# Neighbour attention on one core: the ReLU of the logits moves to GpSimd, the slope to DMA, and 1344 columns of the bar to ScalarE

## The chip, the core and the metric

The program runs on one core of a Trainium2 chip. The metric is the device time of one execution in microseconds. The profile is of one execution on the same chip; its own time stands beside its span.

## The reference

The input x is 32 images of 32 channels and 56 x 56 = 3136 pixels. It is normalised by channel, goes through a convolution with weights of their own at each pixel, and is added to x. What the change touches is the block that follows, on the normalised sum `pts` (3136 points of 32 numbers for each image):

```python
p = pts / norm(pts)
dist = pairwise_distance(p)
_, nn_idx = top_k(-dist, 16)
nbr = pts[nn_idx]
e, e_n = pts @ W_emb + b_emb, nbr @ W_emb + b_emb
logits = leaky_relu(concat(e, e_n) @ W_att + b_att, 0.1)
attn = softmax(logits, over the 16)
agg = sum(nbr * attn)
y = concat(pts, agg) @ W_conv + b_conv
```

A batch normalisation, a ReLU and two additions end it. The logit of a pair is leaky_relu(own + other), where `own` depends on the query alone and `other` on the neighbour alone. Since leaky_relu(v) = 0.1 v + 0.9 max(v, 0) and whatever depends on the query alone drops out of the softmax, a kernel may use 0.1 other + max(0.9 own + 0.9 other, 0), or that less 0.9 own, which is 0.1 other + max(0.9 other, -0.9 own).

## The kernel before

Five stages run one after the other: `normalise_input`, `convolve`, `prepare` (features, unit vectors, and per point the number `share` = 0.1 other), `split_halves`, `attend` and `normalise_output`. Nearly all the time is in `attend`. It has no neighbour lists: for a tile of 128 queries it makes the scores against all 3136 points, finds the 16 best, and gives all other points the weight zero. An image has 25 tiles, so there are 800 tiles, and all engines run the same software pipeline over them (`each_step`). In step s the engines work on these tiles, in the order in which each engine's `body` writes them; each engine takes its instructions strictly in that order, and semaphores join them.

- TensorE scores tile s+1 in two blocks of 1568 columns (L903, L907), adds up a doubt count for tile s (L914), turns the weights of tiles s-3 and s-4 in seven groups (`turn`, L928 and L930; two banks take turns, so a group waits until ScalarE has copied the group two before it), spreads the inverse total (L938) and aggregates tile s-4 (L948). For 7 of an image's 25 tiles it also does the output convolution (L961, L962).
- ScalarE copies the two score blocks (`copy_scores`, L1022), makes the steep part of the logits of tile s+1 from `shares` (`rise`, L1014, a ReLU over 3136 columns), takes the exponential of tile s-1 (L1034) and copies turned groups (L1049).
- VectorE searches the second half of tile s with 7 MAX8 (L1120), masks tile s-1 (`mask`, L1159: logits joined with the bar, and their largest), merges the 14 lists of 8 of tile s into a bound (`merge`, L1181 to L1191, the last of which counts how many scores reach the bound), searches the first half of tile s+1, reads the doubt count (L1126), repairs the tile if the bound is in doubt (L1134 to L1141) and lowers all scores under the bound (`bar`: L1150 for the first 1568 columns, L1151 for the rest, where it also takes in the slope `shares`).
- GpSimd adds the slope `shares` to the first 1568 columns of the logits in two pieces (L875), one beside each of VectorE's searches.
- SP loads an image's data while the one before it is worked on (`load_batch`, 13 transfers), and the features and outputs of four tiles at a time.

`gate(engine, sem, value, passed)` is a wait followed by a semaphore increment. `masked` holds the logits of five tiles, `scores` those of two.

## Time and profile before

| | |
|---|---|
| time, median of 3 runs (lowest to highest) | 11882.48 us (11870.54 to 11883.2) |
| time of the profiled execution | 11878.96 us |
| its span | 11877.3 us |
| VectorE, ScalarE, TensorE, GpSimd busy in the span | 86%, 86%, 75%, 27% |
| moved by DMA in the span | 480.72 MB |

The span is from the first to the last instruction. Busy shares are averages over all stages; the first 1450 us belong to the stages ahead of `attend`, the last 137 us to the one behind it. A group of instructions is told by its line in the kernel, its engine and its tiles.

### The profile page before, as it was taken

The numbers are of one execution on the slowest core, as the hardware profiler recorded it, in microseconds if no ns is written. First come the engines' busy times: TensorE is split into PE (matmuls) and PEld (weight loads), VectorE is DVE, ScalarE is ACT, GpSimd is POOL, SyncE is SP. The second block draws the span as 40 slices with busy tenths as digits, with TensorE's granted clock in tenths as the row PEclk, the third lists the DMA queues.
The fourth block names the chain that finished last, engine by engine and source line by source line (L and its number), as shares of the span: only waits on it lengthen the run. The fifth ranks groups of instructions, "written<-read, shape, count | busy, mean of one in ns | idle before, by whom it ended". The sixth has DMA issues, their size and how long they took to land. (4 is left out here: it accounts for less than half of the span.)

```text
span 11877.3 us, 322193 instructions
## 1 busy us (share of the span) xinstructions
PE 8897.7 (75%) x114762; PEld 6354.6 (54%) x114762; DVE 10249.3 (86%) x23918; ACT 10170.5 (86%) x11593; POOL 3194.5 (27%) x2042
## 2 busy tenths in 40 slices
PE   4885577777777777777777777777777777777775
PEld 3664355555555555555555555555555555555553
DVE  1001599999999999999999999999999999999997
ACT  3332499999999999999999999999999999989986
POOL 1221022222222222222222222222222222222221
PEclk9887799999999999999999999999999999999998
DMA  8666700000000000000000000000000000000003
GB/s 205 172 178 188 223 3 17 17 17 17 17 17 16 17 16 17 17 4 17 17 17 17 17 17 17 17 17 17 17 17 9 12 17 17 17 17 17 17 4 133
DMA packets 220615, 480.72 MB, mean 40 GB/s; under 512 B 139588, under 2 KB 147396, under 8 KB 202436
## 3 DMA queue, kind: packets, MB, share of 16 engines
q1 hardware_dynamic: 196740, 362.84, 12.1%
q0 software_dynamic: 22272, 96.36, 2.6%
q8 instruction: 1023, 16.76, 0.6%
q14 instruction: 580, 4.75, 0.1%
HBM read 353.59 MB, written 105.50 MB: 39 GB/s over the span
## 5 line engine op out<-in xcount | busy, mean ns | idle before, releaser
L875 POOL TENSOR_TENSOR masked<-masked,shares_a 128x784 f32<-128x784 f32 x1600 | 2983.5, 1865 | 7344.5 <-DVE rest L1191 4228.4
L1120 DVE MAX8 found<-scores 128x8 f32<-128x224 f32 x11200 | 3479.7, 371 | 213.9 <-ACT scores L1022 183.4
L1049 ACT ACTIVATE turned_sb<-psum 128x512 f32<-128x512 f32 (+1 forms) x5600 | 2946.4, 573 | 497.2 <-PE psum L928 435.6
L930 PE MATMUL psum<-ident_a,masked 128*128 128x128 f32 x19200 | 2646.9, 282 | 915.9 <-ACT turned_sb L1049 890.7
L930 PEld LDWEIGHTS psum<-ident_a,masked 128*128 128x128 f32 x19200 | 2370.7, 194 | 1370.8 <-issue 1370.5
L1159 DVE CUSTOM_DVE_ANT_0 masked<-masked,scores 128x3136 f32<-128x3136 f32 x800 | 2720.8, 3401 | 0.2 <-DVE scores L1151 0.2
L1022 ACT ACTIVATE scores<-psum 128x1568 f32<-128x1568 f32 x1600 | 2374.4, 1484 | 199.9 <-DVE minus_top L1159 166.2
L1034 ACT ACTIVATE masked<-masked,minus_top 128x3136 f32<-128x3136 f32 x800 | 2363.5, 2954 | 0.0
L1014 ACT ACTIVATE masked<-shares_a,own 128x3136 f32<-128x3136 f32 x800 | 2328.1, 2910 | 1.0
L928 PE MATMUL psum<-ident_a,masked 128*128 128x128 f32 (+1 forms) x10400 | 1759.9, 284 | 533.6 <-ACT turned_sb L1049 500.2
L928 PEld LDWEIGHTS psum<-ident_a,masked 128*128 128x128 f32 (+1 forms) x10400 | 1103.7, 139 | 1292.8 <-issue 1216.2
L903 PE MATMUL psum<-points 32*128 32x392 f32 x12800 | 1543.6, 552 | 28.6 <-DMA rows<-table 16.4
L948 PE MATMUL psum<-turned_sb,rows 128*32 128x128 f32 (+1 forms) x40000 | 1538.8, 282 | 0.5 <-ACT inverse_sb L1030 0.5
L1151 DVE SCALAR_TENSOR_TENSOR scores<-scores,bound,shares_a 128x1568 f32<-128x1568 f32 x800 | 1467.8, 1835 | 0.0
L948 PEld LDWEIGHTS psum<-turned_sb,rows 128*32 128x32 f32 (+1 forms) x40000 | 1148.8, 112 | 271.2 <-issue 174.3
L327 ACT ACTIVATE w_turned<-w_ps 96x384 f32<-96x384 f32 x784 | 348.0, 486 | 592.9 <-PE w_ps L286 588.4
L339 DVE COPY conv_sb<-conv_ps 128x128 f32 x196 | 57.2, 292 | 892.5 <-PE conv_ps L308 892.5
L914 PE MATMUL psum<-ones,above 128*1 128x1 f32 x1600 | 150.8, 163 | 898.0 <-DVE rest L1191 898.0
L1150 DVE TENSOR_SCALAR scores<-scores,bound 128x1568 f32<-128x1568 f32 x800 | 808.6, 1011 | 8.3 <-DVE bound L1141 2.5
L914 PEld LDWEIGHTS psum<-ones,above 128*1 128x1 f32 x1600 | 84.9, 80 | 1156.4 <-issue 1153.3
L903 PEld LDWEIGHTS psum<-points 32*128 32x128 f32 x12800 | 509.7, 186 | 229.2 <-issue 42.8
L907 PE MATMUL psum<-halves_a,minus 3*128 3x392 bf16 x6400 | 566.9, 334 | 0.0
(146 smaller groups left out, 6224.2 us busy)
## 6 DMA issues: line engine op xcount, KB each, us to landing
w_in<-in_L_conv_weight_dram POOLq DMA_DIRECT2D x392, 144.0 KB, 3.4
w_in<-in_L_conv_weight_dram SPq DMA_DIRECT2D x392, 144.0 KB, 3.5
points<-unit SPq DMA_DIRECT2D x128, 392.0 KB
shares_a<-share SPq DMA_DIRECT2D x32, 1568.0 KB
windows<-xg SPq DMA_DIRECT2D x42, 928.0 KB, 13.9
xg<-padded SPq DMA_DIRECT2D x16, 812.0 KB, 18.2
table<-table_sb SPq DMA_DIRECT2D x32, 404.2 KB
rows<-table SPq DMA_DIRECT2D x32, 396.0 KB
```

Source lines behind the costliest of these rows:

```text
L875: nc.gpsimd.tensor_tensor(m, m, shares[:, t.half, k * width:(k + 1) * width], ALU.add).then_inc(logits_ready, 1)
L903: nc.tensor.matmul(ps[:, r * BANK:r * BANK + SCH], points[C * r:C * (r + 1), t.half, t.queries()], points[C * r:C * (r + 1), t.half, at:at ...
L928: last = nc.tensor.transpose(out, block, ident[:])
L930: last = nc.tensor.matmul(out, block, ident[:], start=True, stop=True)
L948: last = nc.tensor.matmul(ps[q:q + C, SUM_BANK:SUM_BANK + P], rows[0:width, t.half, j, 0:C], turned_sb[0:width, t.par, j, :], start=j < PE ...
L1014: nc.scalar.activation(masked[:, t.ring, :], shares[:, t.half, :], ACT.Relu, bias=own[:, t.half, at:at + 1], scale=STEEP / SLOPE).then_inc ...
L1022: nc.scalar.activation(scores[:, t.par, quad * QUAD:(quad + 1) * QUAD].rearrange("p (a b) -> p a b", b=SCH), ps[:, 0:PER * BANK].rearrange ...
L1034: nc.scalar.activation(masked[:, t.ring, :], masked[:, t.ring, :], ACT.Exp, bias=minus_top[:, t.ring:t.ring + 1], scale=-1.0, accum_out=to ...
L1049: nc.scalar.activation(turned_sb[0:high, t.par, g * GROUP:g * GROUP + width // P, :].rearrange("p a b -> p (a b)"), ps[0:high, bank:bank + ...
L1120: n = step(nc.vector.max(found[:, t.par, c, :], scores[:, t.par, c * PART:(c + 1) * PART]))
L1151: nc.vector.scalar_tensor_tensor(high, high, bound[:, 0:1], shares[:, t.half, POOL_COLS:N], ALU.subtract, ALU.min).then_inc(barred, 1)
L1159: nc.vector.tensor_tensor_reduce(m, m, scores[:, t.par, :], -1.0, -NEVER, ALU.add, ALU.min, minus_top[:, t.ring:t.ring + 1]).then_inc(mask ...
```

## The change

GpSimd no longer adds the slope. It makes the logits' steep part itself, from a new per-point row `steep` = 0.9 other that `prepare` stores and SP loads for each image into `steeps` (one buffer, two parts): max(steep, -own) for the first 1792 columns, and its negative, min(-steep, own), for the last 1344, whose `share` and `steep` are stored with the opposite sign. After each of these two operations GpSimd issues a DMA from `shares` that adds the slope into the tile's logits. ScalarE's `rise` is gone. The bar of the last 1344 columns moves from VectorE to ScalarE as a ReLU of bound minus score (`bar_high`); the mask is cut at column 1792 into `mask_low` and `mask_high`; the merge is written out in six calls so that other work stands between them.

```diff
+SPLIT = 4 * CH
@@ prepare: one more row per image in half_sb, stored as steep
-                        nc.tensor.matmul(half_ps[0:2 * PER, c % 4, 0:CH], shares[:], feat_sb[:, par, c * CH:(c + 1) * CH],
+                        nc.tensor.matmul(half_ps[0:ROWS, c % 4, 0:CH],
+                                         shares[:] if c * CH < SPLIT else minus_shares[:], feat_sb[:, par, c * CH:(c + 1) * CH],
@@ attend, SP
+            def load_steep(b, k):
+                cols = SIDES[k]
+                sp.dma_start(steeps[:, cols], steep[bass.ds(b * N + cols.start, cols.stop - cols.start)].partition_broadcast(P)).then_inc(steep_in[k], 16)
...
             def body(tile):
                 here = tile(0)
+                if ends_batch(here):
+                    next_steep(here, 1)
+                if ends_batch(tile(-1)):
+                    next_steep(tile(-1), 0)
@@ attend, GpSimd
-            def add_slope(t, passed):
...
-                    nc.gpsimd.tensor_tensor(m, m, shares[:, t.half, k * width:(k + 1) * width], ALU.add).then_inc(logits_ready, 1)
+            def clamp(t, k):
+                at = t.c if t.c < TILES - 1 else OWN
+                cols = SIDES[k]
+                if k == 0:
+                    nc.gpsimd.tensor_scalar(masked[:, t.ring, cols], steeps[:, cols], -NEVER, minus_own[:, t.half, at:at + 1],
+                                            ALU.min, ALU.max).then_inc(clamped, 1)
+                else:
+                    nc.gpsimd.tensor_scalar(masked[:, t.ring, cols], steeps[:, cols], own[:, t.half, at:at + 1], NEVER,
+                                            ALU.min, ALU.max).then_inc(clamped, 1)
+                gate(pool, clamped, t.count(2, k + 1), pool_passed)
+                pool.dma_start(masked[:, t.ring, cols], shares[:, t.half, cols], accum_op=ALU.add).then_inc(slope_in[t.par], 16)
...
+                if here:
+                    clamp_high(here, tile(1))
+                if coming:
+                    clamp_low(coming, tile(RING - 1), here)
@@ attend, ScalarE
-                nc.scalar.activation(masked[:, t.ring, :], shares[:, t.half, :], ACT.Relu, bias=own[:, t.half, at:at + 1],
-                                     scale=STEEP / SLOPE).then_inc(rises_ready, 1)
+            def bar_high(t):
+                act.wait_ge(settled, t.count(1, 1))
+                s = scores[:, t.par, SPLIT:N]
+                nc.scalar.activation(s, s, ACT.Relu, bias=bound[:, 0:1], scale=-1.0).then_inc(high_barred, 1)
...
                 if older:
                     copy_turned(older, 6)
+                if tile(1):
+                    bar_high(tile(1))
...
-                    rise(coming, tile(RING - 1))
@@ attend, VectorE
-                low, high = scores[:, t.par, 0:POOL_COLS], scores[:, t.par, POOL_COLS:N]
-                step(nc.vector.tensor_scalar(low, low, bound[:, 0:1], 0.0, ALU.subtract, ALU.min))
-                nc.vector.scalar_tensor_tensor(high, high, bound[:, 0:1], shares[:, t.half, POOL_COLS:N],
-                                               ALU.subtract, ALU.min).then_inc(barred, 1)
+                dve.sem_inc(settled, 1)
+                s = scores[:, t.par, 0:SPLIT]
+                nc.vector.tensor_scalar(s, s, bound[:, 0:1], 0.0, ALU.subtract, ALU.min).then_inc(barred, 1)
...
+            def mask_low(t):
+                gate(dve, slope_in[t.par], t.same_par(32, 32), dve_passed)
+                gate(dve, barred, t.count(1, 1), dve_passed)
...
+            def mask_high(t):
+                gate(dve, low_masked, t.count(1, 1), dve_passed)
+                gate(dve, high_barred, t.count(1, 1), dve_passed)
+                m = masked[:, t.ring, SPLIT:N]
+                nc.vector.tensor_tensor_reduce(m, m, scores[:, t.par, SPLIT:N], 1.0, low_top[:, t.par:t.par + 1],
+                                               ALU.add, ALU.min, minus_top[:, t.ring:t.ring + 1]).then_inc(masked_ready, 1)
```

The order of VectorE's instructions in a step of `attend`, from the end of the first search on, before (in brackets the semaphores that an instruction waits for):

```order
L1159 ISA masked,minus_top<-masked,scores 128x3136 [waits a_logits,a_barred]
L1159 ISA minus_top 128x1
L1181 MAX best<-found 128x8 [waits a_chain]
L1183 MATCH_REPLACE rest<-best,found 128x112 [waits a_chain]
L1185 MAX best<-rest 128x8 [waits a_chain]
L1187 SCALAR_TENSOR_TENSOR bound_low<-over,best,margin 128x2 [waits a_chain]
L1189 SCALAR_TENSOR_TENSOR bound<-under,best,bound_low 128x2 [waits a_chain]
L1191 SCALAR_TENSOR_TENSOR rest,above<-found,bound,weight 128x112 [waits a_chain]
```

and in the changed kernel:

```order
L1221 ISA masked,low_top<-masked,scores 128x1792 [waits a_slope0,a_barred]
L1221 ISA low_top 128x1
L1254 MAX best<-found 128x8 [waits a_chain]
L1229 ISA masked,minus_top<-masked,scores,low_top 128x1344 [waits a_low_masked,a_high_barred]
L1229 ISA minus_top 128x1
L1259 MATCH_REPLACE rest<-best,found 128x112 [waits a_chain]
L1243 TENSOR_TENSOR agg<-psum,inverse_sb 128x128 [waits a_summed,a_inverse_in]
L1264 MAX best<-rest 128x8 [waits a_chain]
L1234 RECIPROCAL inverse<-total 128x1 [waits a_exp]
L1269 SCALAR_TENSOR_TENSOR bound_low<-over,best,margin 128x2 [waits a_chain]
L1274 SCALAR_TENSOR_TENSOR bound<-under,best,bound_low 128x2 [waits a_chain]
L1279 SCALAR_TENSOR_TENSOR rest,above<-found,bound,weight 128x112 [waits a_chain]
```

The second mask, with its wait for ScalarE's bar (`a_high_barred`), stands ahead of most of the merge and of the count (L1279). The aggregate's product and the reciprocal, which stood behind the count, now stand ahead of it.

ScalarE in the changed kernel, from the copy of the second score block of one step to the bar of the high side in the next:

```order
L1084 ACTIVATE scores<-psum 128x1568
L1106 REGISTER_ALU
L1111 ACTIVATE turned_sb<-psum 128x512
...
L1111 ACTIVATE turned_sb<-psum 128x512
L1096 ACTIVATE masked,total<-masked,minus_top 128x3136
L1106 REGISTER_ALU
L1111 ACTIVATE turned_sb<-psum 128x512
...
L1111 ACTIVATE turned_sb<-psum 128x512
...
L1111 ACTIVATE turned_sb<-psum 64x128
L1074 ACTIVATE scores<-scores,bound 128x1344
```

The bar (L1074) stands behind the exponential (L1096) and three copies of turned groups; the ReLU over 3136 columns, which stood behind the first score copy, is gone.

TensorE from the doubt count to the second score block of a step, the same in both kernels but for the line numbers, here before:

```order
L914 MATMUL psum<-ones,above 1x1 [waits a_doubt,a_doubts_in]
L37 REGISTER_ALU
L928 MATMUL psum<-ident_a,masked 128x128 [waits a_turned_in]
L928 MATMUL psum<-ident_a,masked 128x128 x3
L938 MATMUL psum<-ident_a,inverse 128x128 [waits a_agg,a_inverse]
L37 REGISTER_ALU
L903 MATMUL psum<-points 128x392 [waits a_scores_in]
L903 MATMUL psum<-points 128x392 x3
L907 MATMUL psum<-halves_a,minus 128x392 x4
```

The doubt product waits for VectorE's count (`a_doubt`), and the second score block stands behind it; nothing moved here.

## Rows read from the trace of the kernel before

**Rows 1.** Busy time by stretch: PE, PEld, DVE, ACT, POOL, PEclk, DMA share, GB/s.

```profile
1450.57:11739.20 10288.63, 7941.34 (x92498) 5612.29 (x92499) 9909.73 (x23244) 9614.67 (x10647) 2978.00 (x1598) 0.97 0.07 15
```

**Rows 2.** One line's instructions: duration min/median/max ns, first and last start.

```profile
L1159 DVE CUSTOM_DVE_ANT_0 masked<-masked,scores x800: 3393/3402/3607, 1450.6 to 11739.2; 128x3136 f32<-128x3136 f32 x160
```

**Rows 3.** In order of time, one step: start us, us, engine, line, [idle before].

```profile
5000.05 3.40 DVE L1159 CUSTOM_DVE_ANT_0 masked<-masked,scores 128x3136 f32<-128x3136 f32 x1
...
5003.69 0.09 DVE L1183 MATCH_VALUE_LOAD rest<-best,found 128x8 f32 x1
...
5004.06 1.47 ACT L1022 ACTIVATE scores<-psum 128x1568 f32<-128x1568 f32 x1
...
5005.15 0.08 DVE L1191 DVE_READ_ACCUMULATOR rest<-found,bound,weight 128x1 f32 x1
...
5005.35 0.15 DVE L1164 RECIPROCAL inverse<-total 128x1 f32<-128x1 f32 x1
...
5005.52 0.19 PE L914 MATMUL psum<-ones,above 128*1 128x1 f32 x2 [1.19 <-DVE rest L1191]
5005.67 0.69 DVE L1120 MAX8 found<-scores 128x8 f32<-128x224 f32 x2 [0.17 <-ACT scores L1022]
...
5007.31 0.35 PE L907 MATMUL psum<-halves_a,minus 3*128 3x392 bf16 x4
...
5008.85 1.50 ACT L1022 ACTIVATE scores<-psum 128x1568 f32<-128x1568 f32 x1
...
5010.20 1.11 ACT L1049 ACTIVATE turned_sb<-psum 128x512 f32<-128x512 f32 x2
...
5011.16 2.96 ACT L1034 ACTIVATE masked<-masked,minus_top 128x3136 f32<-128x3136 f32 x1
...
5012.56 3.40 DVE L1159 CUSTOM_DVE_ANT_0 masked<-masked,scores 128x3136 f32<-128x3136 f32 x1
...
5014.05 1.37 ACT L1049 ACTIVATE turned_sb<-psum 128x512 f32<-128x512 f32 x3
```

**Rows 4.** Groups by line, 5000 to 6000 us: xcount | busy us, mean ns | idle before.

```profile
L875 POOL TENSOR_TENSOR masked<-masked,shares_a 128x784 f32<-128x784 f32 x157 | 292.8, 1865 | 710.2 <-DVE rest L1191 411.8 <-DVE scores L1151 298.5
...
L1014 ACT ACTIVATE masked<-shares_a,own 128x3136 f32<-128x3136 f32 x78 | 227.0, 2910 | 0.1
...
L1151 DVE SCALAR_TENSOR_TENSOR scores<-scores,bound,shares_a 128x1568 f32<-128x1568 f32 x78 | 143.1, 1834 | 0.0
...
L1150 DVE TENSOR_SCALAR scores<-scores,bound 128x1568 f32<-128x1568 f32 x78 | 78.8, 1010 | 0.9 <-DVE bound L1141 0.5
```

**Rows 5.** Groups by line, ScalarE, whole span.

```profile
L1005 ACT ACTIVATE own<-rows,att_bias 128x1 f32<-128x1 f32 x32 | 9.3, 292 | 0.0
```

**Rows 6.** In order of time, a step behind a repaired tile.

```profile
5156.08 0.08 DVE L1191 DVE_READ_ACCUMULATOR rest<-found,bound,weight 128x1 f32 x1
...
5156.46 0.19 PE L914 MATMUL psum<-ones,above 128*1 128x1 f32 x2 [14.21 <-DVE rest L1191]
...
5159.61 0.55 PE L907 MATMUL psum<-halves_a,minus 3*128 3x392 bf16 x4
...
5160.28 1.48 ACT L1022 ACTIVATE scores<-psum 128x1568 f32<-128x1568 f32 x1 [0.91 <-PE psum L907]
```

**Rows 7.** In order of time, TensorE around 3467 us.

```profile
3466.93 2.05 PE L930 MATMUL psum<-ident_a,masked 128*128 128x128 f32 x8 [3.02 <-ACT turned_sb L1049]
```

**Rows 8.** Busy time by stretch, two stretches.

```profile
3466.30:3473.10 6.80, 6.17 (x30) 4.48 (x31) 4.73 (x12) 1.71 (x4) 1.84 (x1) 0.50 0.02 5
...
5145.70:5162.70 17.00, 6.19 (x40) 4.40 (x44) 15.65 (x34) 7.35 (x8) 5.01 (x3) 0.50 0.00 0
```

**Rows 9.** Groups by line, GpSimd, whole span.

```profile
L862 POOL TENSOR_SCALAR_AFFINE_SELECT ident_a<-ident_a 128x128 f32<-128x128 f32 x1 | 0.3, 290 | 73.6 <-DVE own_feat L1091 73.6
```

**Rows 10.** DMA: a queue's packets, MB, share of 16 engines; an issue's KB, us to landing.

```profile
q0 software_dynamic: 22272, 96.36, 2.6%
...
x_sb<-conv POOLq DMA_DIRECT2D x8, 1568.0 KB, 10.4
```

More of the change, by code:

```diff
@@ L342, in _, with prepare @@
             each_half(dve, body)
-def prepare(nc, x, conv, bias, W_emb, W_att, feat, unit, base, half_sq, share, table):
+def prepare(nc, x, conv, bias, W_emb, W_att, feat, unit, base, half_sq, share, steep, table):
     conv_rows, base_rows = conv.rearrange("b c n -> (b c) n"), base.rearrange("b c n -> (b c) n")
@@ L434, in _ @@
                     sp.dma_start(share[rows].rearrange("(b n) -> b n", n=N), half_sb[PER:2 * PER, :]).then_inc(stored[par], 16)
+                    sp.dma_start(steep[rows].rearrange("(b n) -> b n", n=N), half_sb[2 * PER:ROWS, :]).then_inc(stored[par], 16)
             for par in range(2):
@@ L681, in each_step, with attend @@
         fixed(s)
-def attend(nc, feat, unit, pieces, share, table, W_emb, b_emb, W_att, b_att, W_conv, b_conv, y):
+def attend(nc, feat, unit, pieces, share, steep, table, W_emb, b_emb, W_att, b_att, W_conv, b_conv, y):
     BANK = 512
@@ L829, in next_batch, with next_steep, ends_batch @@
                 load_batch(t.batch(1, 1), 1 - t.half)
+            def load_steep(b, k):
+                cols = SIDES[k]
+                sp.dma_start(steeps[:, cols], steep[bass.ds(b * N + cols.start, cols.stop - cols.start)].partition_broadcast(P)).then_inc(steep_in[k], 16)
+            def next_steep(t, k):
+                gate(sp, clamped, t.count(2, k + 1), sp_passed)
+                load_steep(t.batch(1, 1), k)
+            def ends_batch(t):
+                return t and t.c == TILES - 1 and not (isinstance(t.i, int) and t.at > ALL - TILES)
             def load_features(t):
@@ L854, in _ @@
             load_batch(0, 0)
+            for k in range(2):
+                load_steep(0, k)
             each_step(sp, body)
@@ new lines, in clamp_high, with clamp_low @@
+            def clamp_high(t, passed):
+                if t.c == 0:
+                    gate(pool, steep_in[1], t.batch(16, 16), pool_passed)
+                if passed:
+                    gate(pool, barred, passed.count(1, 1), pool_passed)
+                clamp(t, 1)
+            def clamp_low(t, used, beside):
+                if t.c == 0:
+                    gate(pool, steep_in[0], t.batch(16, 16), pool_passed)
+                    gate(pool, own_ready, t.batch(4, 4), pool_passed)
+                if used:
+                    gate(pool, turned, used.count(T_GROUPS, T_GROUPS), pool_passed)
+                if beside:
+                    gate(pool, doubt_ready, beside.count(1, 1), pool_passed)
+                clamp(t, 0)
@@ L881, in _ @@
+            def body(tile):
+                here, coming = tile(0), tile(-1)
+                if here:
+                    clamp_high(here, tile(1))
+                if coming:
+                    clamp_low(coming, tile(RING - 1), here)
             each_step(pool, body)
@@ L1186, in merge, with set_bound @@
                 dve.wait_ge(chain, n)
-                n = step(nc.vector.scalar_tensor_tensor(bound_low[:], over[:], last, margin[:], ALU.mult, ALU.subtract))
+                return step(nc.vector.scalar_tensor_tensor(bound_low[:], over[:], last, margin[:], ALU.mult, ALU.subtract))
+            def set_bound(n):
                 dve.wait_ge(chain, n)
-                n = step(nc.vector.scalar_tensor_tensor(bound[:], under[:], last, bound_low[:], ALU.mult, ALU.min))
+                return step(nc.vector.scalar_tensor_tensor(bound[:], under[:], last, bound_low[:], ALU.mult, ALU.min))
@@ L1190, in merge, with count_above @@
+            def count_above(t, n):
                 dve.wait_ge(chain, n)
-                nc.vector.scalar_tensor_tensor(rest[:], found_all, bound[:, 1:2], weight8[:].rearrange("p a b -> p (a b)"),
+                nc.vector.scalar_tensor_tensor(rest[:], found_of(t), bound[:, 1:2], weight8[:].rearrange("p a b -> p (a b)"),
                                                ALU.is_ge, ALU.mult, accum_out=above[:, 0:1]).then_inc(doubt_ready, 1)
             def body(tile):
-                here, coming = tile(0), tile(-1)
+                here, coming, passed = tile(0), tile(-1), tile(1)
@@ L1196, in body @@
                 if here:
                     n = search(here, 1)
-                if tile(1):
-                    mask(tile(1))
+                if passed:
+                    mask_low(passed)
                 if here:
-                    merge(here, n)
+                    n = top_first(here, n)
+                if passed:
+                    mask_high(passed)
+                if here:
+                    n = drop_first(here, n)
                 if tile(NORM_LAG):
                     normalise(tile(NORM_LAG))
+                if here:
+                    n = top_second(n)
@@ L1204, in body @@
                 if tile(3):
                     invert_total(tile(3))
+                if here:
+                    n = lower_bound(n)
+                    n = set_bound(n)
+                    count_above(here, n)
                 if coming:
@@ L1341, in build @@
     feat, unit = (nc.dram_tensor(name, [C, BATCH * N], FP32).ap() for name in ("feat", "unit"))
-    half_sq, share = (nc.dram_tensor(name, [BATCH * N], FP32).ap() for name in ("half_sq", "share"))
+    half_sq, share, steep = (nc.dram_tensor(name, [BATCH * N], FP32).ap() for name in ("half_sq", "share", "steep"))
     pieces = nc.dram_tensor("pieces", [3, BATCH * N], BF16).ap()
```

109 lines of the change are left out of this document (58 added, 51 removed).

## The prediction

> **What bounds the kernel now.** I read the busy times of the searches first, then the line of the mask, then one regular step in order of time. In the 10,289 us from the first mask to the last VectorE is busy 9,910 us (96%), ScalarE 9,615 (93%), TensorE 7,941 (77%) at a granted clock of 0.97 [rows 1]. The mask on VectorE runs once a step, 800 times, from 1450.6 to 11739.2 us [rows 2]: 799 steps of 12.88 us. One regular step is 12.51 us, from one mask's start to the next, 5000.05 to 5012.56 [rows 3]. The 799 regular steps would take 9,995 us; the other 293 us are repairs, loop ends and batch changes. What lies around the steps is 11,879 (the profiled execution's own time, 3.5 us below the median shown, 11,882.5) minus 10,289, so 1,590 us.
>
> In the regular step VectorE waits 0.17 us for the copied scores and TensorE 1.19 us for the count that VectorE makes [rows 3]. VectorE is the bound, with ScalarE close behind. Of what ScalarE makes in the same step VectorE needs only the score copies. That is what the change alters.
>
> **The change on each engine by itself.** VectorE loses the second half of the bar (1.83 us [rows 4]). Its first half grows from 1568 to 1792 columns, 1.01 x 224/1568 = +0.14 us. The mask is cut in two, one more fixed part of some 0.08 us. From 12.51 - 0.17 that leaves 12.34 - 1.83 + 0.14 + 0.08 = 10.7 us. ScalarE loses the 2.91 us ReLU over 3136 columns and gains one over 1344. Pro rata that is 1.25 us; a one-column activation costs 0.29 us [rows 5], so with the fixed part 0.29 + (2.91 - 0.29) x 1344/3136 = 1.41 us. Ends 1.25 and 1.41; I take 1.41, as these activations have the fixed part. If only these sums counted, the step would fall by 1.7 us.
>
> **The chain that closes.** The new ScalarE order puts the bar of the high side behind the exponential and three copies; the new VectorE order puts the second mask, which waits for that bar, ahead of the rest of the merge and the count; TensorE still waits for the count before the second score block; and ScalarE copies that block before the exponential. So a bar at the head of one ScalarE step leads through VectorE, TensorE and ScalarE to the bar of the next step, and each link waits for the one before it. Its length is the step's least time:
>
> - bar of the high side, 1.41 us;
> - hand-over ScalarE to VectorE, 0.14 us: the copy that begins at 5004.06 ends 1.47 us later, the search starts at 5005.67 [rows 3];
> - second mask to the next instruction, 3.40 x 1344/3136 = 1.46 us [rows 2];
> - from the replace's first part to the count's end, 5003.69 to 5005.15 + 0.08 = 1.54 us, and now also the aggregate's product and the reciprocal that stood behind it (5005.15 to 5005.67 less the 0.17 wait, 0.35 us). They fill gaps of the dependent merge; I keep 0.30 of it: 1.84 us [rows 3];
> - count's end to the end of the second score block on TensorE, 5005.23 to 5007.31 + 0.35 = 2.43 us [rows 3];
> - hand-over TensorE to ScalarE, 0.12 us: 5159.61 + 0.55 to 5160.28 [rows 6];
> - ScalarE: score copy, two turned copies, exponential, three turned copies: 5008.85 to 5014.05 = 5.20 us, and 1.37 us for the three copies less the 0.15 by which an activation starts before the end of the one ahead (5008.85 + 1.50 against 5010.20): 6.42 us [rows 3].
>
> The sum is 13.82 us a step against 12.51. VectorE stands idle in it for some 3 us, between its two masks. Neither the second mask nor anything behind it on VectorE (searches, doubt test, low bar) can pass that wait.
>
> **TensorE's clock on the chain.** From the end of its second turn until the count TensorE has nothing to do. That wait began at 5005.52 - 1.19 = 5004.33; the three copies that stand ahead of the new bar ended a step's 12.51 us before 5014.05 + 1.22, at 5002.76 [rows 3]. Of those 1.57 us I take 1.5. From the bar's start the count takes 1.41 + 0.14 + 1.46 + 1.84 us and TensorE's own start 0.29 (5005.23 to 5005.52). The pause becomes 5.14 - 1.5 = 3.6 us, from 1.19. Before, a wait of 3.02 us [rows 7] was followed by a stretch at 0.50 of the clock, the 1.2 GHz level, that lasted 6.8 us [rows 8]. At that level the link from count to score block takes 5156.08 + 0.08 to 5159.61 + 0.55 = 4.00 us [rows 6, 8], 1.57 more than 2.43. Nothing of it is hidden: in that step ScalarE waits 0.91 us for the block [rows 6]. In 18 of 25 steps nothing fills the pause (in 7 the output convolution stands there), so I charge 18/25 x 1.57 = 1.13 us. Bounds: 0 and 1.57. Step: 13.82 + 1.13 = 14.95 us.
>
> **What I cost at nothing.** GpSimd's two clamps replace two additions of 1.87 us [rows 4]. No row has this operation over these widths. From above, the two-input addition's 2.38 ns a column gives 4.3 and 3.2 us; a one-input operation over 128 columns takes 0.29 us [rows 9], so, if 0.1 us of it is fixed, 1.5 ns a column, 2.8 and 2.1 us, which I take. The first lies beside the second search, the other beside the first search, and VectorE's 3 idle us cover an overrun. The two accumulating DMAs add 128 x 3136 x 4 bytes = 1.606 MB a step. GpSimd's queue moved 96.36 MB in 2.6% of the span of 16 engines, 309 us [rows 10], so plain copying costs 5.15 us a step; one such transfer of 1568 KB took 10.4 us to land beside others. No row shows an accumulating one: below 5.15 there is no reason; above, anything under 15 us is hidden, as a tile's DMAs start over a step before its mask. I take twice, 10.3 us. The Trainium skill ("Collectives: The Full Stack", the bandwidth ceiling) says an add inside a DMA reads two sources and so runs at half the copying rate; by it the price would be this 10.3 us and the sum the same, and it speaks against the fourth case below; no run here shows it. The steep rows are 1.6 MB per batch in front of the batch loads in SP's queue; their cover is the step between a batch's last clamp and the next first one, and uncovered they would cost 32 x 10.4 = 333 us. The two further small activations per batch (0.3 us each) fall into ScalarE's wait for the score block.
>
> **The sum.** 1,590 + 293 + 799 x 14.95 = 13,828 us. I keep the 293 us whole, though VectorE's idle time will swallow part of them. That is 1,949 us above the profiled execution.
>
> **The rivals.**
>
> 1. *The chain holds, the clock doesn't fall.* For it: score blocks and turns still give TensorE some 9 us of work a step. Against it: the fall behind a 3.02 us wait [rows 7, 8]. 1,883 + 799 x 13.82 = 12,925 us.
> 2. *Faster: the chain doesn't close*, because the high bar is ready before VectorE asks. VectorE's 10.7 us then set the step: 1,883 + 799 x 10.7 = 10,432 us. It decides if ScalarE runs ahead by more than the 3 us by which the bar comes late in my sum, that is, if count to score block and exponential to bar together were 3 us shorter than their rows. Only the sums by engine speak for it.
> 3. *The clamps hold VectorE up.* If a clamp and a VectorE operation on two inputs exclude each other, and the clamps cost the upper price, then low bar 1.15 (1.01 x 1792/1568), clamp 3.2, mask 1.94, maximum 0.3, mask 1.46, merge 1.84, clamp 4.3 and two hand-overs of 0.14 follow each other: 14.5 us, 1,883 + 799 x 14.5 = 13,469 us, with no share of the clock's in it. At the price that I take they come to 11.9 us and decide nothing. The Trainium skill ("SBUF — State Buffer", who interferes with whom) states this lock: whichever starts first holds the shared port for its whole instruction. In the traces so far no clamp-like operation overlaps a two-input one for long, so nothing shows it.
> 4. *The accumulating DMAs set the step.* Point of decision: 14.95/5.15, 2.9 times the copying price. At four times it, 20.6 us a step, 18,342 us. For it: no such transfer was ever seen here.
>
> **How the numbers follow.** The forecast gets 0.62, the first rival 0.20, the second 0.04, the third 0.05, the fourth 0.09. Forecast at its clock bounds: 13.82 to 15.39, which is 12,925 to 14,180 us; errors of 0.2 us in the chain add 160 us on either side. The range 12,750 to 14,400 us holds the forecast, rivals 1 and 3, and leaves out rivals 2 and 4. This kernel's runs differ by 0.1%, so 0.2% (24 us) is about what can be told from no change. Faster by more than that: rival 2, 0.04. Same: 0.01, if errors cancel. Slower: 0.95.
>
> **What would show it.** Right: ScalarE waiting for the score block with 1.5 us or more before the second score copy; VectorE waiting 2 to 4 us before the second mask, released by the high bar; TensorE waiting 3.5 to 4.5 us before the doubt product; a mean granted clock in the searches below 0.9; a step of 14.5 to 15.5 us. Wrong: a step under 12.5 us with VectorE busy throughout (rival 2); a wait before the first mask that the DMA ends (rival 4); masks or bars stretched beyond the durations here (rival 3); the clock at 0.97 as before, and a step near 13.8 (rival 1).

## The result and the profile after

The changed kernel takes 14,166.9 us, median of 4 runs (14,157.99 to 14,183.73), against 11,882.8 (11,870.54 to 11,888.83) for the kernel before, run beside it: 1.1925 times as long, 95% interval 1.1905 to 1.1946, or 2,284 us more. The prediction was slower, 13,828 us, with a range that holds the time. The profiled execution took 14,157.99 us.

First the searches as a whole, from the first low mask to the last, as [rows 1] shows them for before:

```profile
core 0: us, PE busy (x) PEld busy (x) DVE busy (x) ACT busy (x) POOL busy (x), PEclk, DMA share, GB/s
1455.30:14014.40 12559.10, 9618.03 (x92440) 6722.86 (x92440) 8600.81 (x24042) 8588.39 (x10707) 3940.57 (x3192) 0.82 0.58 119
```

VectorE did shed the work that the change takes from it: 8,601 us instead of 9,910. So did ScalarE: 8,588 instead of 9,615. Over 799 steps that is 10.76 and 10.75 us a step. Yet the stretch is 2,270 us longer. VectorE and ScalarE are each busy 68% of it, TensorE 77% (9,618 us, part of them at a lower clock). No engine is busy throughout; something makes them wait for each other. The mask's line, which answers to [rows 2], gives the step:

```profile
engine op xcount: duration ns min/median/max, first and last start us, forms
L1221 DVE CUSTOM_DVE_ANT_0 masked<-masked,scores x800: 2001/2006/2027, 1455.3 to 14014.4; 128x1792 f32<-128x1792 f32 x160
```

(14,014.4 - 1,455.3) / 799 = 15.72 us a step, 12.88 before. The waits of the whole run, longest first, say who waits for whom (engine, line waited at, releaser, us in total, times, longest):

```profile
POOL masked L908 <- DVE rest L1279: 7435.3, 799, 16.1
...
PE psum L975 <- DVE rest L1279: 2589.1, 800, 16.5
DVE masked L1229 <- ACT scores L1074: 2202.1, 785, 10.2
...
ACT scores L1084 <- PE psum L968: 1346.2, 802, 17.9
```

Read as arrows these close a ring. VectorE's second mask (L1229) waits for ScalarE's bar (L1074); TensorE's doubt product (L975) waits for VectorE's count (L1279); ScalarE's score copy (L1084) waits for TensorE's score block (L968); and the bar stands behind that copy in ScalarE's order. Each of the three waits occurs some 800 times, about once a step. The first line looks worst and costs nothing here: GpSimd is early and has time.

The ring can be followed through two steps in order of time (start, duration, engine, line; in brackets the idle time before and what ended it):

```profile
6000.89 1.62 DVE L1229 CUSTOM_DVE_ANT_0 masked<-masked,scores,low_top 128x1344 f32<-128x1344 f32 x1 [3.20 <-ACT scores L1074]
...
6003.95 0.08 DVE L1279 DVE_READ_ACCUMULATOR rest<-found,bound,weight 128x1 f32 x1
...
6004.33 0.19 PE L975 MATMUL psum<-ones,above 128*1 128x1 f32 x2 [3.66 <-DVE rest L1279]
...
6006.43 0.57 PE L968 MATMUL psum<-halves_a,minus 3*128 3x392 bf16 x4
...
6007.18 1.48 ACT L1084 ACTIVATE scores<-psum 128x1568 f32<-128x1568 f32 x1 [1.44 <-PE psum L968]
...
6013.85 1.40 ACT L1074 ACTIVATE scores<-scores,bound 128x1344 f32<-128x1344 f32 x1
...
6015.44 1.62 DVE L1229 CUSTOM_DVE_ANT_0 masked<-masked,scores,low_top 128x1344 f32<-128x1344 f32 x1 [2.36 <-ACT scores L1074]
...
6018.50 0.08 DVE L1279 DVE_READ_ACCUMULATOR rest<-found,bound,weight 128x1 f32 x1
...
6018.88 0.19 PE L975 MATMUL psum<-ones,above 128*1 128x1 f32 x2 [3.66 <-DVE rest L1279]
...
6021.75 0.55 PE L968 MATMUL psum<-halves_a,minus 3*128 3x392 bf16 x4
...
6022.50 1.48 ACT L1084 ACTIVATE scores<-psum 128x1568 f32<-128x1568 f32 x1 [1.83 <-PE psum L968]
...
6028.57 0.60 ACT L1111 ACTIVATE turned_sb<-psum 128x512 f32<-128x512 f32 x1 [0.24 <-PE psum L991]
...
6029.83 0.27 ACT L1111 ACTIVATE turned_sb<-psum 64x128 f32<-64x128 f32 x1 [0.67 <-PE psum L989]
6030.01 1.40 ACT L1074 ACTIVATE scores<-scores,bound 128x1344 f32<-128x1344 f32 x1
...
6031.60 1.62 DVE L1229 CUSTOM_DVE_ANT_0 masked<-masked,scores,low_top 128x1344 f32<-128x1344 f32 x1 [3.20 <-ACT scores L1074]
```

The first step, mask to mask, takes 14.55 us, the second 16.16. The links do the same work in both. What differs is TensorE's clock, in the same stretch cut into pieces (columns as above; the clock is the third figure from the end):

```profile
6000.67:6004.33 3.66, 0.00 (x0) 0.03 (x1) 3.37 (x13) 2.35 (x4) 0.07 (x1) 1.00 0.00 0
6004.33:6005.60 1.27, 1.21 (x12) 1.02 (x16) 1.27 (x7) 0.14 (x1) 1.27 (x1) 1.00 0.03 6
6005.60:6008.90 3.30, 3.30 (x20) 2.02 (x16) 1.83 (x4) 1.86 (x3) 1.98 (x3) 0.53 0.16 33
6008.90:6015.15 6.25, 6.24 (x88) 4.75 (x87) 4.17 (x10) 6.08 (x8) 1.62 (x2) 0.98 0.99 196
...
6018.88:6021.75 2.87, 2.81 (x16) 1.73 (x20) 2.87 (x9) 0.28 (x1) 2.29 (x2) 0.60 0.00 0
6021.75:6024.24 2.49, 2.49 (x17) 1.79 (x9) 0.15 (x2) 1.74 (x2) 1.91 (x3) 0.50 0.69 138
6024.24:6028.00 3.76, 3.76 (x60) 3.23 (x60) 3.76 (x8) 3.76 (x5) 0.67 (x1) 0.73 1.11 218
```

In both steps TensorE idles 3.66 us with the clock granted in full. When it works again the clock at first stays at 1.00 (to 6005.60 and beyond in the first step, to 6019.40 in the second) and then falls to 0.50, the 1.2 GHz level; a piece that holds both levels shows their mean. Behind the second pause the low stretch is the longer one: 0.50 until 6026.00, 1.00 again from 6026.30. It slows the aggregate that stands ahead of the turns (L1009, 2.81 us instead of 1.95), so that the turns begin later and ScalarE's copies wait for them.

The new instructions on GpSimd, by group (count, busy us, mean ns, idle before), and its DMA queue (packets, MB, share of 16 engines' span), beside [rows 9, 10]:

```profile
L914 POOL DMA_DIRECT2D masked<-shares_a x1600 | 1423.5, 890 | 974.0 <-POOL masked L908 455.8 <-POOL masked L911 454.7 <-issue 39.0
L908 POOL TENSOR_SCALAR masked<-steeps,minus_own 128x1792 f32<-128x1792 f32 x800 | 1395.8, 1745 | 7462.3 <-DVE rest L1279 7435.3 <-ACT minus_own L1067 27.0
L911 POOL TENSOR_SCALAR masked<-steeps,own 128x1344 f32<-128x1344 f32 x800 | 1151.2, 1439 | 210.7 <-DVE scores L1214 162.1 <-issue 30.9
...
q0 software_dynamic: 252672, 1380.97, 48.1%
```

The clamps take 1.75 and 1.44 us. Together with the DMA issues GpSimd is busy 4.93 us a step. The first mask waits for the adding DMAs 24 us in the whole run.

### The profile page after: what moved, and what is told of

The parts are those of the page before. It is cut to its first block and busy times, and to the rows that moved or that the text cites. A ratio compares the mean times of both kernels' runs of the same rounds, so it can differ in the third digit from the quotient of the medians.

```text
span 14156.3 us, 333305 instructions
## 1 busy us (share of the span) xinstructions
PE 10574.8 (75%) x114762; PEld 7465.9 (53%) x114762; DVE 8939.9 (63%) x24731; ACT 9142.2 (65%) x11658; POOL 4160.9 (29%) x3642
## 5 line engine op out<-in xcount | busy, mean ns | idle before, releaser
L908 POOL TENSOR_SCALAR masked<-steeps,minus_own 128x1792 f32<-128x1792 f32 x800 | 1395.8, 1745 | 7462.3 <-DVE rest L1279 7435.3
L991 PEld LDWEIGHTS psum<-ident_a,masked 128*128 128x128 f32 x19200 | 2844.6, 228 | 888.9 <-issue 886.9
L991 PE MATMUL psum<-ident_a,masked 128*128 128x128 f32 x19200 | 3219.6, 321 | 79.7 <-issue 72.0
L1084 ACT ACTIVATE scores<-psum 128x1568 f32<-128x1568 f32 x1600 | 2352.6, 1470 | 1400.9 <-PE psum L968 1346.2
L1229 DVE CUSTOM_DVE_ANT_0 masked<-masked,scores,low_top 128x1344 f32<-128x1344 f32 x800 | 1294.4, 1618 | 2204.1 <-ACT scores L1074 2202.1
L1096 ACT ACTIVATE masked<-masked,minus_top 128x3136 f32<-128x3136 f32 x800 | 2330.6, 2913 | 0.0
L975 PE MATMUL psum<-ones,above 128*1 128x1 f32 x1600 | 150.6, 163 | 2589.1 <-DVE rest L1279 2589.1
L989 PE MATMUL psum<-ident_a,masked 128*128 128x128 f32 (+1 forms) x10400 | 1872.2, 305 | 257.5 <-ACT turned_sb L1111 200.5
L964 PE MATMUL psum<-points 32*128 32x392 f32 x12800 | 1991.4, 700 | 24.6 <-DMA rows<-table 16.0
L1009 PE MATMUL psum<-turned_sb,rows 128*32 128x128 f32 (+1 forms) x40000 | 1866.3, 328 | 0.5 <-ACT inverse_sb L1092 0.5
L914 POOL DMA_DIRECT2D masked<-shares_a x1600 | 1423.5, 890 | 974.0 <-POOL masked L908 455.8
L989 PEld LDWEIGHTS psum<-ident_a,masked 128*128 128x128 f32 (+1 forms) x10400 | 1202.3, 150 | 942.7 <-issue 850.4
L1221 DVE CUSTOM_DVE_ANT_0 masked<-masked,scores 128x1792 f32<-128x1792 f32 x800 | 1605.5, 2007 | 24.5 <-DMA masked<-shares_a 24.3
L1009 PEld LDWEIGHTS psum<-turned_sb,rows 128*32 128x32 f32 (+1 forms) x40000 | 1409.5, 134 | 389.1 <-issue 300.1
L975 PEld LDWEIGHTS psum<-ones,above 128*1 128x1 f32 x1600 | 91.0, 80 | 2856.6 <-issue 2856.6
L911 POOL TENSOR_SCALAR masked<-steeps,own 128x1344 f32<-128x1344 f32 x800 | 1151.2, 1439 | 210.7 <-DVE scores L1214 162.1
L1074 ACT ACTIVATE scores<-scores,bound 128x1344 f32<-128x1344 f32 x800 | 1122.2, 1403 | 48.0 <-DVEq L1208 48.0
L1214 DVE TENSOR_SCALAR scores<-scores,bound 128x1792 f32<-128x1792 f32 x800 | 902.8, 1128 | 18.8 <-DVE bound L1204 3.1
```

The lines of the kernel that those rows point to most:

```text
L908: nc.gpsimd.tensor_scalar(masked[:, t.ring, cols], steeps[:, cols], -NEVER, minus_own[:, t.half, at:at + 1], ALU.min, ALU.max).then_inc(cl ...
L914: pool.dma_start(masked[:, t.ring, cols], shares[:, t.half, cols], accum_op=ALU.add).then_inc(slope_in[t.par], 16)
L964: nc.tensor.matmul(ps[:, r * BANK:r * BANK + SCH], points[C * r:C * (r + 1), t.half, t.queries()], points[C * r:C * (r + 1), t.half, at:at ...
L989: last = nc.tensor.transpose(out, block, ident[:])
L991: last = nc.tensor.matmul(out, block, ident[:], start=True, stop=True)
L1009: last = nc.tensor.matmul(ps[q:q + C, SUM_BANK:SUM_BANK + P], rows[0:width, t.half, j, 0:C], turned_sb[0:width, t.par, j, :], start=j < PE ...
```

## The experiments

All times are medians; ratios are to the kernel before, run beside them. Every diff is against the changed kernel, unless it says otherwise.

### The change without its last part

The bar of the high side returns to VectorE; the rest of the change stays.

```diff
@@ ScalarE
-                if tile(1):
-                    bar_high(tile(1))
@@ VectorE, bar
-                dve.sem_inc(settled, 1)
+                s = scores[:, t.par, SPLIT:N]
+                nc.vector.tensor_scalar(s, s, bound[:, 0:1], 0.0, ALU.subtract, ALU.min).then_inc(high_barred, 1)
@@ VectorE, mask_high: the sum times -1 instead of 1; prepare and clamp: the high side's sign as the low side's
```

> The high bar goes back to VectorE, behind the low bar's place (all logits with one sign, all of the mask as a sum times -1); clamps, adding DMAs and the cut mask stay. It is the change without its last part. Theory: VectorE gets some 0.87 us more a step, 11.5, and loses the wait; the loop second search to count 7.6, score block 2.4, score copy 1.5, hand-overs 0.4 gives 11.9 us, more if the clock falls: 11,100 to 11,900 us. If the clamps or the DMAs cost the time and not the bar on ScalarE: 13,500 us or more.

Measured: 11,665.6 us, ratio 0.9821 (0.9806 to 0.9836). Clamps on GpSimd and slope by DMA are a gain of 209 us (1.8%) over the kernel before that ran beside it (11,874.6), clear of the noise. The last part of the change, the bar on ScalarE, is what costs: 14,167 - 11,666 = 2,501 us.

### The clock alone

```diff
             def add_doubts(t):
+                for _ in range(10):
+                    nc.tensor.matmul(ps[96:P, Y_BANK:Y_BANK + P], ident[:, 0:C], ident[:], start=True, stop=True)
                 gate(pe, doubt_ready, t.count(1, 1), pe_passed)
```

> Ten extra products of the identity (128 x 32 by 128 x 128), whose result nobody reads, stand on TensorE ahead of the doubt product, where it waits 3.66 us for the count; all else as in the change. Theory (chain and clock are two terms): granted clock over 0.95, the links from count to score block and ScalarE's turned copies back at full-clock values, step 1.40 + 0.19 + 1.54 + 1.60 + 2.43 + 0.18 + 6.42 = 13.76 us, 12,600 to 12,900 us in all. If the clock costs nothing on the chain: 14,100 to 14,200 us. If the clock stays at the low level all the same, the ten products take longer than the wait and the time rises, by up to 500 us.

Measured: 13,014.6 us, ratio 1.0951 (1.0933 to 1.0969). Ten products more a step, and 1,152 us less. In this kernel the lines behind the insertion have numbers two higher. One step in order of time:

```profile
6009.39 1.40 ACT L1076 ACTIVATE scores<-scores,bound 128x1344 f32<-128x1344 f32 x1
...
6010.98 1.62 DVE L1231 CUSTOM_DVE_ANT_0 masked<-masked,scores,low_top 128x1344 f32<-128x1344 f32 x1 [2.14 <-ACT scores L1076]
...
6014.05 0.08 DVE L1281 DVE_READ_ACCUMULATOR rest<-found,bound,weight 128x1 f32 x1
...
6014.43 0.19 PE L977 MATMUL psum<-ones,above 128*1 128x1 f32 x2 [1.21 <-DVE rest L1281]
...
6016.22 0.35 PE L968 MATMUL psum<-halves_a,minus 3*128 3x392 bf16 x4
...
6016.76 1.48 ACT L1086 ACTIVATE scores<-psum 128x1568 f32<-128x1568 f32 x1 [0.92 <-PE psum L968]
...
6023.21 1.40 ACT L1076 ACTIVATE scores<-scores,bound 128x1344 f32<-128x1344 f32 x1
...
6024.80 1.62 DVE L1231 CUSTOM_DVE_ANT_0 masked<-masked,scores,low_top 128x1344 f32<-128x1344 f32 x1 [2.14 <-ACT scores L1076]
```

And the whole of its searches:

```profile
1464.00:12878.10 11414.10, 9664.41 (x108444) 7231.44 (x108448) 8620.65 (x24042) 8518.64 (x10709) 4019.49 (x3192) 0.98 0.64 131
```

The clock is 0.98 instead of 0.82, and the step from mask to mask is 24.80 - 10.98 = 13.82 us, with VectorE's wait for the bar still there. So the ring is there without the clock's fall, and the fall comes on top. The total lies 115 us above the range expected: the mean step is 11,414 / 799 = 14.29 us. Most of the 0.47 us over the regular step are irregular steps, which I had left almost out. The rest are the products themselves. In the 218 of the 799 steps in which the output convolution (L1024, L1025 here) stands ahead of the doubt product, TensorE has no pause left to fill, the products run past the count, and the step takes 14.27 us in the median instead of 13.82: some 100 us in all. So the 1,152 us are what the products save on balance, and the clock's fall cost some 100 us more than that (an estimate from these steps).

### What the adding DMAs cost

First they were left out, then they copied instead of adding.

```diff
-                pool.dma_start(masked[:, t.ring, cols], shares[:, t.half, cols], accum_op=ALU.add).then_inc(slope_in[t.par], 16)
+                pool.sem_inc(slope_in[t.par], 16)
```

> The accumulating DMAs of the slope are left out (1600 in all, 1.28 GB), so the logits lack their part 0.1 other; GpSimd frees their waiters itself. Theory: the first mask waits for these DMAs 24 us in the whole run, so nothing changes by more than 30 us: 14,130 to 14,200 us. If the DMAs' traffic slows the engines or holds the step: below 13,900 us.

```diff
-                pool.dma_start(masked[:, t.ring, cols], shares[:, t.half, cols], accum_op=ALU.add).then_inc(slope_in[t.par], 16)
+                pool.dma_start(masked[:, t.ring, cols], shares[:, t.half, cols]).then_inc(slope_in[t.par], 16)
```

> The 1600 adding DMAs copy instead of adding, so the logits are the slope alone. All else as in the change: it prices the add. If adding reads both sources at half the rate, the queue's share of the 16 engines falls from 48% to about 25% of the span; the trace's plain transfers on this queue ask for 5.15 us a step, 800 x 5.15 / 14,150 = 29%, and some 2% for the earlier stages. Time as in the change within 100 us if the DMAs bind nothing.

Measured: 14,094.0 us without them (1.1866, 1.1846 to 1.1886), and 14,081.1 us with copies (one run). 73 us are more than the 30 expected, but 3% of the loss: the DMAs don't hold the step. The queue line of the copying kernel:

```profile
q0 software_dynamic: 252672, 1380.97, 24.7%
```

The same packets and bytes take half the time. 0.481 x 14,156 less the 309 us of the other stages [rows 10] is 6,500 us, 8.13 us a step; copying, 0.247 x 14,079 - 309 = 3,169 us, 3.96 us a step. An add costs 2.05 copies. The Trainium skill ("Collectives: The Full Stack", the bandwidth ceiling) derives half the rate for the adds of a ring collective, as an add reads two sources; the two runs agree for these DMAs inside one core, with the factor 2.05.

### The bar one step earlier

```diff
@@ ScalarE, body
-                if tile(1):
-                    bar_high(tile(1))
...
+                if tile(0):
+                    bar_high(tile(0))
                 if tile(1):
                     exponentiate(tile(1))
```

> ScalarE's bar of the high side is made one step earlier, just ahead of the exponential, instead of at the head of the next step. Theory: the exponential and three copies leave the path to the second mask. The count still comes behind both masks, so the loop that is left is second search to count 7.6 us, count to score block 2.4, hand-overs 0.4, score copy 1.5: 11.9 us, more where the clock falls. 799 x 12.2 + 1,599 = 11,350 us, between 11,100 and 12,000 us; VectorE's wait before the second mask falls below 0.5 us. If DMA or GpSimd set the step: 14,170 us. If ScalarE now waits for VectorE's doubt test and passes that wait on, over 13,000 us.

Measured: 12,324.9 us, ratio 1.0372 (1.0349 to 1.0395). The wait for the bar is gone, as expected (7 us in all instead of 2,202), and 1,842 us with it. But the time is 325 us over the range. In the trace another wait has grown: TensorE's turns (L989) wait 1,862 us for ScalarE's turned copies, 201 in the change. The copies of the last three groups stand behind the exponential, which now comes later, and TensorE has two banks for seven groups. TensorE is now the late one: it waits for the count (L975) in 62 steps, in the change in 800. The clock is 0.89.

To see how much of that was the clock, the ten products were put into this kernel as well.

> The early bar together with the ten extra products on TensorE. It tells what the early bar's 12,325 us held of clock: theory (the chain left is 11.9 us at full clock, the rest is the clock): 1,599 + 293 + 799 x 11.9 = 11,400 us, between 11,250 and 11,650. If a wait of another kind lengthened it, it stays over 12,000 us.

Measured: 13,404.1 us, ratio 1.1284 (1.1266 to 1.1301), 1,079 us more instead of some 900 less: a clear miss. The trace says why:

```profile
6009.47 0.08 DVE L1281 DVE_READ_ACCUMULATOR rest<-found,bound,weight 128x1 f32 x1
...
6010.29 2.85 PE L973 MATMUL psum<-ident_a 128*32 128x128 f32 x17
...
6012.87 0.19 PE L977 MATMUL psum<-ones,above 128*1 128x1 f32 x2
...
6013.52 0.15 DVE L1191 TENSOR_SCALAR doubts<-psum 1x1 uint32<-1x1 f32 x1 [1.95 <-PE psum L977]
```

The count is ready at 6009.55 and TensorE begins the products only at 6010.29: it comes late from its turns and has no pause ahead of the doubt product here. The products lie on the path: VectorE waits 909 us in all for the doubt product, 91 without them. They raise the clock (0.96) and cost more than that gives. So this run does not tell how much of the early bar's 12,325 us is clock; it tells that TensorE with its turns is on its path.

### The second mask behind the count

This takes the bar out of the path to the count. `bound` needs a second buffer, since ScalarE may still read one tile's bound while VectorE writes the next.

```diff
-        bound = enter(nc.sbuf_tensor("bound", [P, 2], FP32))
+        bound = enter(nc.sbuf_tensor("bound", [P, 2, 2], FP32))
@@ bar, bar_high, set_bound, count_above, settle_doubts: bound[:, t.par, ...]
@@ VectorE, body
-                if passed:
-                    mask_high(passed)
...
                     count_above(here, n)
+                if passed:
+                    mask_high(passed)
```

> Second mask (1344 columns) moved behind the count on VectorE; the bound has two buffers, so that ScalarE's bar of one tile may still read while VectorE writes the next tile's bound. Theory (closed chain): bar 1.40, hand-over 0.19 and second mask 1.54 us leave the path to the count. VectorE's own 10.65 us a step and the loop second search to count (7.6 less 1.6), score block 2.4, score copy 1.5, hand-overs 0.4 (10.3 us) are then the longest; with what ScalarE's order still costs 10.8 to 11.8 us a step, and with 1,599 us outside the steps and up to 293 of irregular ones 10,300 to 11,300 us, below the kernel before. TensorE's wait for the count falls below 2 us, granted clock above 0.95. If the adding DMAs or GpSimd set the step: 14,100 us.

Measured: 11,419.7 us, ratio 0.9615 (0.9602 to 0.9628). One instruction in another place turns 19% slower into 4% faster. It is 120 us above the expected range. Two steps of the second mask and the low clamp:

```profile
6004.97 1.62 DVE L1229 CUSTOM_DVE_ANT_0 masked<-masked,scores,low_top 128x1344 f32<-128x1344 f32 x1
6005.09 3.13 POOL L908 TENSOR_SCALAR masked<-steeps,minus_own 128x1792 f32<-128x1792 f32 x1 [3.00 <-PE psum L991]
...
6017.51 1.75 POOL L908 TENSOR_SCALAR masked<-steeps,minus_own 128x1792 f32<-128x1792 f32 x1 [3.66 <-PE psum L991]
...
6017.62 3.05 DVE L1229 CUSTOM_DVE_ANT_0 masked<-masked,scores,low_top 128x1344 f32<-128x1344 f32 x1 [0.34 <-ACT scores L1074]
```

Both now begin at the count. Whichever is first keeps its own time (1.62 or 1.75 us), and the other takes 1.4 us longer than its own, as if it began when the first had ended. This is the lock of the prediction's third rival, seen for the first time. The Trainium skill ("SBUF — State Buffer", who interferes with whom) describes just this for VectorE with two inputs against a reading GpSimd; the four rows agree.

So the clamp was made to wait for the mask instead of the count (against the late-mask kernel):

```diff
-            def clamp_low(t, used, beside):
+            def clamp_low(t, used, passed):
...
-                if beside:
-                    gate(pool, doubt_ready, beside.count(1, 1), pool_passed)
+                if passed:
+                    gate(pool, masked_ready, passed.count(1, MASKED_FREE + 1), pool_passed)
```

> The late mask, and GpSimd's clamp of the low side waits for the end of the second mask and not for the count. In the late-mask kernel count, clamp and second mask begin together, and of the two one takes its own time and the other 1.4 us more (mask 1.62 and clamp 3.13, or clamp 1.75 and mask 3.05 us); the mask's mean is 1.94 us. Theory (the two exclude each other on the shared memory port): mask back to 1.62 in all steps, low clamp back to 1.75, the 0.32 us a step are VectorE's: up to 256 us less than 11,420, between 11,150 and 11,400 us. If the stretch comes from something else (DMA writes, for one): the mask's mean stays above 1.8 us and the time at 11,420.

```profile
L1229 DVE CUSTOM_DVE_ANT_0 masked<-masked,scores,low_top x800: 1617/1619/1620, 1460.6 to 11247.6; 128x1344 f32<-128x1344 f32 x160
```

All 800 masks are back to 1.62 us, so the lock it was. But the time is 11,384.0 us (0.9588, 0.9575 to 0.9601): 36 us of a possible 256. The rest turned into another wait: VectorE's waits for ScalarE's score copies and bars grew from 475 to 722 us.

That other wait was taken to be ScalarE's, 1.32 us ahead of the second score copy, for a block that itself waits for the first score copy. A turned copy was moved into it (against the clamp-gate kernel):

```diff
+                if past:
+                    copy_turned(past, 2)
                 if coming:
                     copy_scores(coming, 1, tile(1))
                 if past:
-                    copy_turned(past, 2)
                     copy_turned(past, 3)
```

> As the clamp-gate kernel, and on ScalarE the third turned copy stands ahead of the second score copy instead of behind it. In the late-mask kernel ScalarE waits there 1.32 us for the score block, which waits on TensorE for the first score copy (the two blocks share their banks). Theory: ScalarE's order sets what is left over VectorE's 10.65 us; some 0.48 us of copying move into the wait: up to 380 us less than the clamp-gate kernel, 10,800 to 11,200 us. If ScalarE sets nothing any more, the same time as the clamp-gate kernel.

Measured: 11,124.2 us, ratio 0.9369 (0.9356 to 0.9382), 260 us less, and ScalarE's waits for the score blocks fell from 715 to 354 us. This is the fastest kernel here that leaves nothing out: 6.3% less than before, 21% less than the change. Its mean step is (10,972.0 - 1,451.6) / 799 = 11.92 us, against 10.79 of VectorE's work (8,625 us in the same stretch).

Last, the adding DMAs were left out of this kernel too (the same edit as above).

> The fastest order so far (late mask, clamp gate, third turned copy ahead of the score copy) with the adding DMAs left out, so that the logits lack their part 0.1 other. It asks what these DMAs cost once the chain no longer hides them. In the kernel with them the first mask waits for them 261 us in 61 places, at the changes of batch. Theory: that wait goes, and little else, since other waits close up behind: 100 to 260 us less than 11,124, so 10,860 to 11,020 us. If the DMAs stay hidden as in the change itself, 11,040 to 11,130 us; if their traffic slows the engines, below 10,860.

Measured: 10,711.8 us, ratio 0.9014 (0.8999 to 0.9030): 412 us less, more than the 261 us that the mask waits for these DMAs, and outside the expected range. It falls where I had expected it if the traffic slowed the engines, but the traces don't show that: from the first low mask to the last VectorE is busy 8,625 us in both kernels, and ScalarE 8,474 and 8,451. So the rest, too, should be waits that follow from the first (ScalarE's score copies wait 219 us for the delayed mask, and the clock is 0.98 instead of 0.96); which of them make up the sum was not separated.

## Why the prediction was right, and where it was off

**The account.** Before to the change without its last part, 11,883 to 11,666: -217 us (209 where both ran side by side). The bar on ScalarE with the clock held up by the products, 11,666 to 13,015: +1,349, of which some 100 are the products' own. The clock's fall, less these 100, 13,015 to 14,167: +1,152. Together +2,284.

**The engines by themselves** were right: VectorE's 10.7 us a step came out as 10.76.

**The chain** was right in its form and to the hundredth in its sum, partly by luck, as the links show (us; with the products is the kernel of the clock experiment):

| link | predicted | with the products | after, first step | after, second step |
|---|---|---|---|---|
| second mask to the count's end | 1.46 + 1.84 = 3.30 | 3.15 | 3.14 | 3.14 |
| count to the end of the score block | 2.43 | 2.44 | 2.97 | 3.72 |
| hand-over to ScalarE | 0.12 | 0.19 | 0.18 | 0.20 |
| ScalarE, score copy to the bar | 6.42 | 6.45 | 6.67 | 7.51 |
| bar and hand-over | 1.41 + 0.14 | 1.59 | 1.59 | 1.59 |
| sum | 13.82 | 13.82 | 14.55 | 16.16 |

The merge was 0.24 us too dear, as nearly all of the aggregate's product and the reciprocal fits into its gaps (12.53 to 14.13, 1.60 us instead of 1.84); the second mask (0.09) and the two hand-overs (0.12) were together about as much too cheap.

**The clock term** is the term that was mis-sized. I charged 18/25 x 1.57 = 1.13 us a step; the products saved 1,152 / 799 = 1.44, and the clock itself cost more. The reason was right: the pause grew to 3.66 us (3.6 predicted), and the clock fell, to 0.82 in the mean. What failed is the charge of nothing for the 7 of 25 steps in which the output convolution stands in the pause. Step for step against the kernel with the products, from mask to mask, the 581 steps without the convolution lost 1.64 us in the mean, close to my 1.57. But the 218 steps with it lost 0.89, although the products lengthen them by 0.45 in the kernel that they are compared with. The convolution did not keep the clock up here. This is the step that follows the two above, with its convolution (L1022, L1023) from 6031.31 to 6033.32, and two pieces of it:

```profile
6035.04 0.19 PE L975 MATMUL psum<-ones,above 128*1 128x1 f32 x2 [1.72 <-DVE rest L1279]
...
6037.13 0.57 PE L968 MATMUL psum<-halves_a,minus 3*128 3x392 bf16 x4
...
6037.88 1.48 ACT L1084 ACTIVATE scores<-psum 128x1568 f32<-128x1568 f32 x1 [1.43 <-PE psum L968]
...
6046.14 1.62 DVE L1229 CUSTOM_DVE_ANT_0 masked<-masked,scores,low_top 128x1344 f32<-128x1344 f32 x1 [2.37 <-ACT scores L1074]
```

```profile
6036.00:6038.00 2.00, 2.00 (x15) 0.85 (x14) 1.94 (x5) 0.40 (x2) 1.42 (x2) 0.63 0.00 0
6038.00:6040.00 2.00, 2.00 (x16) 1.76 (x19) 0.50 (x2) 2.00 (x3) 1.61 (x2) 0.52 0.84 168
```

TensorE still idles 1.72 us before the doubt product, the clock falls behind it as in the other steps, and the step takes 14.54 us. In the steps without the convolution the sum came out near by luck: the link from count to score block took 2.97 and 3.72 us, not the 4.00 of [rows 6], which stood behind a wait of 14.21 us, and ScalarE's own part, where I had nothing, grew from 6.45 to 6.67 and 7.51, because the low clock outlasts the link and delays the turns. Nearly all of the 0.41 us a step by which 13,828 fell short of the profiled 14,158 (330 us) is therefore clock, most of it in the steps with the convolution. The irregular steps were about right: I kept 0.37 us a step for them; in the kernel with the products they come to 0.47 less the some 0.12 that the products themselves cost.

**What I cost at nothing** cost next to nothing here (73 us without the adding DMAs): the clamps took 1.75 and 1.44 us (2.8 and 2.1 taken), the adding DMAs 8.13 us a step (10.3 taken: my copying price, 5.15, was too high, and the factor of two right).

**The rivals.** The first, the chain without the clock's fall, did not happen, but the experiment that made it happen gave 13,015 us where 12,925 was worked out. The second is excluded by VectorE's 785 waits for the bar. The third: in all 800 steps of the change the second mask lasted 1617 to 1621 ns, the first 2001 to 2027 and the low bar 1122 to 1155, so no lock held them there; the late mask showed that the lock exists as soon as the order puts the two side by side, though taking it away gained only 36 us. The fourth is excluded by the two DMA runs.

**The signs** came nearly as listed: VectorE waits 2.8 us a time for the bar, TensorE 3.66 us in steps without the convolution, and the clock is 0.82. ScalarE waits 1.44 and 1.83 us for the score block in the two steps, where I had said 1.5 or more, and the mean step, 15.72, is above the 14.5 to 15.5 given, irregular steps included.

## What to carry to other kernels

Work moved to another engine can cost more than it frees when other engines wait for it in its new place: follow each new wait through every engine's fixed order, and if the arrows come back to the moved instruction, add up the links. Here that sum, 13.82 us at the full clock, was the regular step, though VectorE had 10.76 us of work. An opened ring may need no more than one instruction put behind another (here the mask behind the count, and a second buffer of two numbers a partition). And the longer idle stretch of TensorE was paid twice here, the second time when it worked on at the lower clock, down to the engines that wait for its later work; other work in that stretch, like the output convolution, did not by itself prevent it.

## What was not expected

- Filling an idle stretch with products whose result nobody reads made the program 8% faster (14,167 to 13,015 us) where TensorE waited, and 9% slower (12,325 to 13,404 us) where it did not. What differed was whether TensorE waited at that line.
- Two steps with the same 3.66 us pause had low-clock stretches of different length: behind the first the clock is 0.98 in the mean from 6008.90 on, behind the second it is still 0.50 until 6026.00. One took 14.55, the other 16.16 us.
- The adding DMAs are worth 73 us in the slow kernel and 412 in the fast one. A cost that a slow ring hides comes back once the ring is open.
